# Macaron block in fp32 on one core: the low half of the gated product is subtracted on GpSimd instead of VectorE

## The chip, the cores and the metric

The kernel runs on one core of one Trainium2 chip. The metric is the device time of one execution in microseconds (us). Four engines work here: TensorE (PE) multiplies matrices, VectorE (DVE), ScalarE (ACT) and GpSimd (POOL) do the elementwise work, and SyncE (SP) issues the DMAs. Each runs its own instructions in order and waits on semaphores for the others.

## What is computed

Three sublayers over x of 4 batches by 512 tokens by 512 features, all in fp32:

```
x = x + 0.5 * ffn(layernorm(x))
x = x + scan_layer(layernorm(x))
x = x + 0.5 * ffn(layernorm(x))

ffn(x):         silu(x @ w_gate.T) * (x @ w_up.T) @ w_down.T            # hidden size 2048
scan_layer(x):  z = x @ W.T;  m_k[t] = lam_k * m_k[t-1] + z[t], k = 0..3
                h = z + sum_k eta_k * m_k;  gamma * layernorm(h) + beta
```

The product silu(gate) * up is called the gated product below; in the kernel it is the buffer `hid`.

## The kernel before

**Precision by two halves.** TensorE multiplies here in a rounded fp32 format. So each operand is split in a high half (the rounded copy, made on ScalarE) and a low half (the operand minus its high half, a subtraction), and each product is made of three matmuls: high by high, high by low, low by high. The helper `three` issues them (L718, L719, L720).

**Passes and steps.** A tile is one batch of 512 tokens. Each of the 4 tiles goes twice through the feed-forward network, which makes 8 passes, and a pass has 16 steps, one for each slice of 128 hidden units. In step g, with global number g, TensorE does in this order: the matmuls of gate(g) (12 of them), of up(g) (12), and then those of down(g-1) (12), that is, the down product of the slice before. Its PSUM banks `gate_ps` and `up_ps` are single. So up(g) waits until VectorE has read the bank of the step before (`hid_done`).

**The gated product.** After gate(g), ScalarE writes silu(gate) into `hid` (L409). After up(g), VectorE multiplies it by `up_ps` in place (L658, counts `hid_done`). ScalarE copies the result to the high half `hid_hi` (L426, counts `hid_hi_ready`), and VectorE subtracts to get the low half `hid_lo` (L667, counts `hid_lo_ready`). down(g) waits for `hid_lo_ready`. All three buffers have two slots.

**Work beside the steps.** `beside` tells what else a step carries:
- "ln" or "pre", 4 steps of a pass: VectorE takes the layer norm of 128 tokens each (statistics, then a reciprocal root by a one-column power on GpSimd, L448, then `norm`), turns them in blocks, and VectorE and ScalarE place the blocks in `row_t`. ScalarE then makes `xt_hi` (L391), VectorE `xt_lo` (L547), the operands of a later pass.
- "scan", 5 steps (s = 0 to 4), once for each tile: in steps s = 0 to 3, TensorE also makes one unit of z = x @ W.T, 12 matmuls into `aux_ps`, which come last in the step, after down(g-1). Their weights are split in the same step: ScalarE copies `w_scan_hi` (L418) right behind the silu, GpSimd subtracts `w_scan_lo` (L482). VectorE's part of unit s, the function `scan` (four recurrences L558, four accumulations L562, a transpose L590 and the placing), stands at the end of step s, and the gated product of step s+1 behind it.
- "post", 5 steps: the second half of the scan layer (norm, gamma, beta, residual) and the layer norm for the tile's second pass, with two one-column powers on GpSimd for each step (L454, L448).

In pass 0, ScalarE and GpSimd also split all the weights of the feed-forward network, a slice per step: GpSimd subtracts 128x1024 (`gu_lo`, L461) and 128x512 (`dn_lo`, L475). The halves are kept in HBM, and later passes fetch them.

**What sets the order.** All orders are written out by hand: the function `step(c)` of each engine is called by the same walk over all steps. SP issues the next weights of the FFN, and in scan steps also the next W (`load_w_scan`), which waits for `w_scan_lo_ready`.

Of the kernel before, what the change touches and what calls it, by code (L numbers as in the profile page):

```python
# [28 lines left out]
F32 = mybir.dt.float32  # L29
F32R = mybir.dt.float32r  # L30
ALU = mybir.AluOpType
# [16 lines left out]
def macaron_kernel(nc, x_in, w_ffn_in, w_scan_in, lam_logit_in, eta_in, gamma_in, beta_in, out):  # L48
# [18 lines left out]
    with ExitStack() as ctx:  # L67
        def sb(name, shape, dt=F32):
            return ctx.enter_context(nc.sbuf_tensor(name, shape, dt))

        def sem(name):
            return ctx.enter_context(nc.semaphore(name))
# [16 lines left out]
        hid = sb("hid", [P, 2, tokens])  # L89
        hid_hi = sb("hid_hi", [P, 2, tokens], F32R)  # L90
        hid_lo = sb("hid_lo", [P, 2, tokens], F32R)
# [43 lines left out]
        def parts(eng, c):  # L135


            split = P // 4 if c.beside == "post" and c.s < ST else P // 2
            return range(0, split, SQ) if eng is nc.vector else range(split, P, SQ)

        def place_rows(copy, parts):

            place_blocks(copy, parts, rows[:, 1, :], row_t, 0, blocks_placed)
# [40 lines left out]
        down_done = sem("down_done")  # L184
        silu_done = sem("silu_done")
        hid_done = sem("hid_done")
        hid_hi_ready = sem("hid_hi_ready")
        hid_lo_ready = sem("hid_lo_ready")
# [22 lines left out]
        def wait(eng, semaphore, n):  # L211

            if isinstance(n, int) and n <= 0:
                return
            eng.wait_ge(semaphore, n)

        def ln_count(f):

            return f - ST + 3
# [223 lines left out]
        @block.gpsimd  # L443
        def _(pool):
            def ln(f, u):

                pool.wait_ge(ln_ve_done, ln_count(f))
                pool.tensor_tensor(ln_rstd[:, u:u + 1], ln_ve[:, u:u + 1], minus_half[:, 0:1], ALU.pow  # L448
                                   ).then_inc(ln_rstd_done, 1)

            def post_norm(n):

                pool.wait_ge(post_ve_done, n + 1)
                pool.tensor_tensor(post_rstd[:, :], post_ve[:, :], minus_half[:, 0:1], ALU.pow  # L454
                                   ).then_inc(post_rstd_done, 1)

            def split_gu(t, slot, g):


                pool.wait_ge(gu_hi_ready, g + 1)  # L460
                pool.tensor_tensor(gu_lo[:, slot, :], w_ffn[:, t, 0:GU], gu_hi[:, slot, :].bitcast(F32),  # L461
                                   ALU.subtract).then_inc(gu_lo_ready, 1)

            def step(c):
                g = c.p * HT + c.t
                if c.beside in ("ln", "pre"):
                    ln(c.f, c.sp)
                if c.beside == "post" and c.s < ST:
                    post_norm(c.tile * ST + c.s)
                if isinstance(c.p, int) and c.p == 0:  # L470
                    if not (isinstance(c.t, int) and c.t == LAST):
                        split_gu(c.t + 1, (c.tp + 1) % 2, g + 1)

                    pool.wait_ge(dn_hi_ready, g + 1)
                    pool.tensor_tensor(dn_lo[:, c.tp, :], w_ffn[:, c.t, GU:GU + D],  # L475
                                       dn_hi[:, c.tp, :].bitcast(F32), ALU.subtract).then_inc(dn_lo_ready, 1)
                if c.beside == "post" and c.s < ST:
                    ln(c.f, c.sp)
                if c.beside == "scan" and c.s < DT:

                    pool.wait_ge(w_scan_hi_ready, c.tile * DT + c.s + 1)
                    pool.tensor_tensor(w_scan_lo[:, :], w_scan[:, :], w_scan_hi[:, :].bitcast(F32),  # L482
                                       ALU.subtract).then_inc(w_scan_lo_ready, 1)

            pool.memset(ident[:, :], 0.0).then_inc(ident_zero, 1)
            pool.memset(minus_half[:, :], -0.5).then_inc(ident_zero, 1)

            pool.wait_ge(ident_zero, 2)
            pool.affine_select(out=ident[:, :], in_=ident[:, :], compare_op=ALU.not_equal, fill=1.0, base=0,
                               pattern=[[-1, P]], channel_multiplier=1).then_inc(ident_ready, 1)  # L490
            for u in range(0, ST, 2):

                pool.wait_ge(ln_ve_done, u // 2 + 1)
                pool.tensor_tensor(ln_rstd[:, u:u + 2], ln_ve[:, u:u + 2], minus_half[:, u:u + 2], ALU.pow
                                   ).then_inc(ln_rstd_done, 1)
            pool.wait_ge(gate0_hi_ready, 1)
            pool.tensor_tensor(gu_lo[:, 0, 0:DT * P], w_ffn[:, 0, 0:DT * P], gu_hi[:, 0, 0:DT * P].bitcast(F32),
                               ALU.subtract).then_inc(gate0_lo_ready, 1)
            pool.wait_ge(gu_hi_ready, 1)
            pool.tensor_tensor(gu_lo[:, 0, DT * P:GU], w_ffn[:, 0, DT * P:GU],  # L500
                               gu_hi[:, 0, DT * P:GU].bitcast(F32), ALU.subtract).then_inc(gu_lo_ready, 1)
            walk(pool, step)

        @block.vector
        def _(dve):
            def stats(f, u, x):

                dve.bn_stats(ln_stats[:, u, :], x)

                dve.drain()  # L510
                dve.bn_aggr(ln_mv[:, u, :], ln_stats[:, u, :]).then_inc(ln_mv_done, 1)
                dve.wait_ge(ln_mv_done, f + 1)
                dve.tensor_scalar(ln_ve[:, u:u + 1], ln_mv[:, u, 1:2], EPS, None, ALU.add).then_inc(ln_ve_done, 1)

            def norm(f, u, x, row):


                dve.wait_ge(ln_rstd_done, ln_count(f))
                dve.tensor_scalar(row, x, ln_mv[:, u, 0:1], ln_rstd[:, u:u + 1], ALU.subtract,
                                  ALU.mult).then_inc(row_ready, 1)  # L520

            def turn_blocks(f):


                dve.wait_ge(row_ready, f + 1)

                dve.wait_ge(xt_hi_ready, f)
                dve.transpose(rows[:, 1, :], rows[:, 0, :]).then_inc(blocks_turned, 1)  # L528

                dve.drain()  # L530
# [97 lines left out]
            def add_y(p, b):  # L628


                dve.wait_ge(down_done, (p + 1) * HT)
                for q in range(ST):
                    x = x_tok[:, b * ST + q, :]
                    dve.scalar_tensor_tensor(x, down_ps[q][:, :], 0.5, x, ALU.mult, ALU.add).then_inc(y_added, 1)

            def step(c):
                g = c.p * HT + c.t
                if c.beside == "ln":

                    for b in (1,) if isinstance(c.p, int) and c.p == 0 else range(2, tiles):  # L640
                        dve.wait_ge(x_arrived[b], 16)
                if c.beside == "post":
                    post(c)
                if c.beside == "pre":

                    dve.drain()
                if c.beside in ("ln", "pre"):
                    x = x_tok[:, c.tile * ST + c.s, :]
                    stats(c.f, c.sp, x)
                    norm(c.f, c.sp, x, rows[:, 0, :])  # L650
                    turn_blocks(c.f)
                    place_rows(dve.tensor_copy, parts(nc.vector, c))
                if c.beside == "post" and c.s == ST:
                    split_xt(c, 1 - c.odd)

                dve.wait_ge(silu_done, g + 1)
                dve.wait_ge(up_done, g + 1)
                dve.tensor_tensor(hid[:, c.tp, :], hid[:, c.tp, :], up_ps[:, :], ALU.mult).then_inc(hid_done, 1)  # L658
                if c.beside == "post" and c.s < ST:

                    dve.drain()
                    stats(c.f, c.sp, x_tok[:, c.tile * ST + c.s, :])
                    split_xt(c, 1 - c.odd)

                dve.wait_ge(hid_hi_ready, g + 1)
                wait(dve, down_done, g - 1)
                dve.tensor_tensor(hid_lo[:, c.tp, :], hid[:, c.tp, :], hid_hi[:, c.tp, :].bitcast(F32),  # L667
                                  ALU.subtract).then_inc(hid_lo_ready, 1)
                if isinstance(c.t, int) and c.t == 0 and c.done is not None:
                    add_y(c.p - 1, c.done)  # L670
                if c.beside in ("ln", "pre"):
                    split_xt(c, 1 - c.odd)
                if c.beside == "scan" and c.s < DT:
                    scan(c)
# [180 lines left out]
```

## Time and profile before

| | |
|---|---|
| median of 3 runs | 1171.23 us (1169.49 to 1172.03) |
| the profiled execution | 1167.63 us, of which its span, first to last instruction, 1165.8 us |
| TensorE matmuls busy | 1121.0 us, 96% of the span |
| VectorE busy | 618.1 us, 53% |
| ScalarE busy | 372.5 us, 32% |
| GpSimd busy | 123.9 us, 11% |
| mean granted TensorE clock | 0.987 |

TensorE has work nearly always, so a change to another engine can win only what TensorE still waits for, and can lose wherever it makes TensorE wait anew.

### The profile page before, as it was taken

To read this page: it belongs to the slowest core of one execution; us is meant where nothing else is said; L and a number is where in the kernel's file an instruction comes from. 1 tells how busy PE (TensorE), PEld (TensorE's weight loads), DVE (VectorE), ACT (ScalarE), POOL (GpSimd) and SP (SyncE) were. 2 spreads that over 40 slices of the span, in tenths; PEclk is the share of its full clock that TensorE was granted. 3 is DMA by queue.
4 is the path that set the end of the run, shared out by engine and by line. 5 is a ranking of instruction groups with operands and counts; after the bars stand their busy time and mean duration, and the time that the engine had idled before them with its cause. 6 is when DMAs were issued, how large, how long until landed. Compare 5 with 4: busy or idle time off the path is not lost.

```text
span 1165.8 us, 14814 instructions
## 1 busy us (share of the span) xinstructions
PE 1121.0 (96%) x4860; PEld 914.1 (78%) x4860; DVE 618.1 (53%) x1244; ACT 372.5 (32%) x884; POOL 123.9 (11%) x118
## 2 busy tenths in 40 slices
PE   8998999989999999998999999999899998999998
PEld 7777888868877887886887888788688786887777
DVE  4842146788561115588946111559885588931112
ACT  4633324235251113332534111332362432521111
POOL 4434400101000000010100000001010010100000
PEclk9999999999999999998999999999899998999999
DMA  8889455444555546453544555553355452564544
GB/s 339 286 306 334 199 203 204 168 152 163 191 188 177 195 181 240 164 188 118 196 184 178 201 177 201 210 214 140 142 180 212 167 189 109 191 221 177 205 166 158
DMA packets 46564, 227.70 MB, mean 195 GB/s; under 512 B 5168, under 2 KB 5168, under 8 KB 30128
## 3 DMA queue, kind: packets, MB, share of 16 engines
q1 hardware_dynamic: 46368, 227.04, 53.1%
q8 instruction: 29, 0.48, 0.2%
q14 instruction: 23, 0.19, 0.0%
q10 hardware_dynamic: 144, 0.00, 0.0%
HBM read 197.66 MB, written 29.36 MB: 195 GB/s over the span
## 4 chain that ended last, share of the span: by engine, by line
PE 60%; DMA 15%; DVE 14%; issue 6%; POOL 2%; SPq 2%; ACT 1%; DVEq 0%; POOLq 0%; ACTq 0%
DMA gu<-gu_kept 13%; PE up_ps L718 7%; PE up_ps L719 7%; PE up_ps L720 7%; PE down_ps L718 7%; PE down_ps L720 7%; PE down_ps L719 6%; PE gate_ps L718 6%; PE gate_ps L719 6%; PE gate_ps L720 6%; DVE rows L558 5%; DVE scan_sum L562 4%; DVE scan_tok L132 2%; DMA gu_kept<-gu 2%; PE gate_ps L776 1%
## 5 line engine op out<-in xcount | busy, mean ns | idle before, releaser
L658 DVE TENSOR_TENSOR hid<-hid,up_ps 128x512 f32<-128x512 f32 x128 | 88.0, 687 | 380.2 <-PE up_ps L720 368.2
L718 PE MATMUL up_ps<-xt_hi,gu 128*128 128x512 f32 x512 | 204.4, 399 | 22.9 <-DVE hid L658 22.9
L718 PE MATMUL gate_ps<-xt_hi,gu 128*128 128x512 f32 x480 | 190.8, 397 | 13.2 <-DMA gu<-gu_kept 8.9
L719 PE MATMUL up_ps<-xt_lo,gu 128*128 128x512 f32 x512 | 203.1, 397 | 0.0
L720 PE MATMUL up_ps<-xt_hi,gu 128*128 128x512 f32 x512 | 202.9, 396 | 0.0
L409 ACT ACTIVATE hid<-gate_ps 128x512 f32<-128x512 f32 x128 | 76.7, 599 | 393.5 <-PE gate_ps L720 368.1
L718 PE MATMUL down_ps<-dn,hid_hi 128*128 128x512 f32 x512 | 199.8, 390 | 0.0
L719 PE MATMUL down_ps<-dn,hid_hi 128*128 128x512 f32 x512 | 199.4, 389 | 0.0
L720 PE MATMUL down_ps<-dn,hid_lo 128*128 128x512 f32 x512 | 199.2, 389 | 0.0
L719 PE MATMUL gate_ps<-xt_lo,gu 128*128 128x512 f32 x480 | 187.7, 391 | 0.0
L720 PE MATMUL gate_ps<-xt_hi,gu 128*128 128x512 f32 x480 | 187.6, 391 | 0.0
L426 ACT CAST hid_hi<-hid 128x512 fp32r<-128x512 f32 x128 | 79.5, 621 | 213.1 <-DVE hid L658 213.1
L667 DVE TENSOR_TENSOR hid_lo<-hid,hid_hi 128x512 fp32r<-128x512 f32 x128 | 92.2, 720 | 83.8 <-ACT hid_hi L426 83.8
L718 PEld LDWEIGHTS up_ps<-xt_hi,gu 128*128 128x128 f32 x512 | 98.2, 192 | 48.5 <-issue 28.4
L132 ACT COPY row_t<-rows 32x128 f32<-32x128 f32 x400 | 118.9, 297 | 28.0 <-DVE rows L528 22.4
L718 PEld LDWEIGHTS gate_ps<-xt_hi,gu 128*128 128x128 f32 x480 | 90.5, 189 | 43.3 <-DMA gu<-gu_kept 12.2
L720 PEld LDWEIGHTS up_ps<-xt_hi,gu 128*128 128x128 f32 x512 | 98.4, 192 | 21.0
L719 PEld LDWEIGHTS up_ps<-xt_lo,gu 128*128 128x128 f32 x512 | 98.4, 192 | 20.2
L718 PEld LDWEIGHTS down_ps<-dn,hid_hi 128*128 128x128 f32 x512 | 96.6, 189 | 20.2
L719 PEld LDWEIGHTS down_ps<-dn,hid_hi 128*128 128x128 f32 x512 | 96.5, 188 | 20.2
L720 PEld LDWEIGHTS down_ps<-dn,hid_lo 128*128 128x128 f32 x512 | 96.3, 188 | 20.1
L720 PEld LDWEIGHTS gate_ps<-xt_hi,gu 128*128 128x128 f32 x480 | 90.5, 189 | 19.2
(68 smaller groups left out, 946.1 us busy)
## 6 DMA issues: line engine op xcount, KB each, us to landing
gu<-gu_kept SPq DMA_DIRECT2D x112, 1024.0 KB, 5.9
dn<-dn_kept SPq DMA_DIRECT2D x112, 512.0 KB, 3.5
gu_kept<-gu SPq DMA_DIRECT2D x16, 1024.0 KB, 8.3
w_ffn<-w_ffn_in SPq DMA_DIRECT2D x15, 768.0 KB, 6.4
dn_kept<-dn SPq DMA_DIRECT2D x16, 512.0 KB, 3.0
w_scan<-w_scan_in SPq DMA_DIRECT2D x16, 256.0 KB, 3.9
x_tok<-x_in SPq DMA_DIRECT2D x3, 1024.0 KB, 10.3
out<-x_tok SPq DMA_DIRECT2D x3, 1024.0 KB, 6.3
```

The source lines that it names most:

```text
L132: last = copy(dst[b:b + SQ, :, at + a:at + a + SQ], blocks[a:a + SQ, :, b:b + SQ])
L409: act.activation(hid[:, c.tp, :], gate_ps[:, :], ACT.Silu).then_inc(silu_done, 1)
L426: act.copy(hid_hi[:, c.tp, :], hid[:, c.tp, :]).then_inc(hid_hi_ready, 1)
L558: return dve.tensor_tensor_scan(rows[:, k % 2, :], lam[:, k:k + 1].to_broadcast([P, tokens]), z, 0.0, ALU.mult, ALU.add)
L562: return dve.scalar_tensor_tensor(total, rows[:, k % 2, :], eta[:, k:k + 1], to, ALU.mult, ALU.add)
L658: dve.tensor_tensor(hid[:, c.tp, :], hid[:, c.tp, :], up_ps[:, :], ALU.mult).then_inc(hid_done, 1)
L667: dve.tensor_tensor(hid_lo[:, c.tp, :], hid[:, c.tp, :], hid_hi[:, c.tp, :].bitcast(F32), ALU.subtract).then_inc(hid_lo_ready, 1)
L718: pe.matmul(dst, a_hi, b_hi, start=start, stop=False)
L719: pe.matmul(dst, a_hi, b_lo, start=False, stop=False)
L720: return pe.matmul(dst, a_lo, b_hi, start=False, stop=stop)
L776: pe.matmul(dst[:, cols], gu[:, c.tp, w[k]], xt_hi[:, c.odd, k, cols], start=k == 0 and gu is gu_hi, stop=False)
```

## The change

The subtraction that gives `hid_lo` is taken out of VectorE's step and put in GpSimd's step with the same two waits: behind the weight splits of pass 0, ahead of the second layer-norm power of a "post" step, and ahead of the subtraction for `w_scan_lo` of a "scan" step. Nothing else differs. There are 128 such subtractions.

```
--- before.py
+++ after.py
@@ -474,6 +474,11 @@
                     pool.wait_ge(dn_hi_ready, g + 1)
                     pool.tensor_tensor(dn_lo[:, c.tp, :], w_ffn[:, c.t, GU:GU + D],
                                        dn_hi[:, c.tp, :].bitcast(F32), ALU.subtract).then_inc(dn_lo_ready, 1)
+
+                pool.wait_ge(hid_hi_ready, g + 1)
+                wait(pool, down_done, g - 1)
+                pool.tensor_tensor(hid_lo[:, c.tp, :], hid[:, c.tp, :], hid_hi[:, c.tp, :].bitcast(F32),
+                                   ALU.subtract).then_inc(hid_lo_ready, 1)
                 if c.beside == "post" and c.s < ST:
                     ln(c.f, c.sp)
                 if c.beside == "scan" and c.s < DT:
@@ -661,11 +666,6 @@
                     dve.drain()
                     stats(c.f, c.sp, x_tok[:, c.tile * ST + c.s, :])
                     split_xt(c, 1 - c.odd)
-
-                dve.wait_ge(hid_hi_ready, g + 1)
-                wait(dve, down_done, g - 1)
-                dve.tensor_tensor(hid_lo[:, c.tp, :], hid[:, c.tp, :], hid_hi[:, c.tp, :].bitcast(F32),
-                                  ALU.subtract).then_inc(hid_lo_ready, 1)
                 if isinstance(c.t, int) and c.t == 0 and c.done is not None:
                     add_y(c.p - 1, c.done)
                 if c.beside in ("ln", "pre"):
```

GpSimd's program in the five scan steps of the first tile and the start of the post steps, before the change (x4 is four in a row; each row ends with the semaphores that it waits for):

```order
L482 TENSOR_TENSOR w_scan_lo<-w_scan,w_scan_hi 128x512 [waits w_scan_hi_ready] x4
L454 TENSOR_TENSOR ln_rstd<-ln_ve,minus_half 128x1 [waits post_ve_done]
L448 TENSOR_TENSOR ln_rstd<-ln_ve,minus_half 128x1 [waits ln_ve_done]
L454 TENSOR_TENSOR ln_rstd<-ln_ve,minus_half 128x1 [waits post_ve_done]
L448 TENSOR_TENSOR ln_rstd<-ln_ve,minus_half 128x1 [waits ln_ve_done]
```

The same place with the change:

```order
L480 TENSOR_TENSOR hid_lo<-hid,hid_hi 128x512 [waits down_done,hid_hi_ready]
L487 TENSOR_TENSOR w_scan_lo<-w_scan,w_scan_hi 128x512 [waits w_scan_hi_ready]
...
L480 TENSOR_TENSOR hid_lo<-hid,hid_hi 128x512 [waits down_done,hid_hi_ready]
L487 TENSOR_TENSOR w_scan_lo<-w_scan,w_scan_hi 128x512 [waits w_scan_hi_ready]
L480 TENSOR_TENSOR hid_lo<-hid,hid_hi 128x512 [waits down_done,hid_hi_ready]
L454 TENSOR_TENSOR ln_rstd<-ln_ve,minus_half 128x1 [waits post_ve_done]
L480 TENSOR_TENSOR hid_lo<-hid,hid_hi 128x512 [waits down_done,hid_hi_ready]
L448 TENSOR_TENSOR ln_rstd<-ln_ve,minus_half 128x1 [waits ln_ve_done]
```

Each subtraction for `w_scan_lo` now stands behind the `hid_lo` of its own step, and so does each layer-norm power of the post steps (L448).

VectorE's program from the gated product of a scan step to that of the next (the recurrences of L558 are listed as SCALAR_TENSOR_TENSOR here), before:

```order
L658 TENSOR_TENSOR hid<-hid,up_ps 128x512 [waits up_done,silu_done]
L667 TENSOR_TENSOR hid_lo<-hid,hid_hi 128x512 [waits down_done,hid_hi_ready]
L558 SCALAR_TENSOR_TENSOR rows<-lam,aux_ps 128x512 [waits z_done,rows_arrived]
...
L590 STREAM_TRANSPOSE row_t<-scan_sum 128x512
L132 COPY scan_tok<-row_t 32x4x32 x8
L658 TENSOR_TENSOR hid<-hid,up_ps 128x512 [waits up_done,silu_done]
```

and with the change:

```order
L663 TENSOR_TENSOR hid<-hid,up_ps 128x512 [waits up_done,silu_done]
L563 SCALAR_TENSOR_TENSOR rows<-lam,aux_ps 128x512 [waits z_done,rows_arrived]
...
L595 STREAM_TRANSPOSE row_t<-scan_sum 128x512
L132 COPY scan_tok<-row_t 32x4x32 x8
L663 TENSOR_TENSOR hid<-hid,up_ps 128x512 [waits up_done,silu_done]
```

The recurrence follows the gated product directly; its own wait, for TensorE's z, is the same.

## Rows read from the trace of the kernel before

**Rows 1.** The page: busy us of each engine, its share of the span, instructions.

```profile
PE 1121.0 (96%) x4860; PEld 914.1 (78%) x4860; DVE 618.1 (53%) x1244; ACT 372.5 (32%) x884; POOL 123.9 (11%) x118
```

**Rows 2.** Who waited for whom: us in total, times, longest us.

```profile
PE up_ps L718 <- DVE hid L658: 22.9, 13, 3.9
```

**Rows 3.** DVE timeline, first scan stage: start us, us, line, operation, idle before.

```profile
205.27 0.69 DVE L658 TENSOR_TENSOR hid<-hid,up_ps 128x512 f32<-128x512 f32 x1 [5.40 <-PE up_ps L720]
...
210.71 2.33 DVE L558 TENSOR_TENSOR_SCAN rows<-lam,aux_ps 128x512 f32<-128x512 f32 x2 [3.37 <-PE aux_ps L720]
...
222.08 0.69 DVE L658 TENSOR_TENSOR hid<-hid,up_ps 128x512 f32<-128x512 f32 x1
...
224.07 2.32 DVE L558 TENSOR_TENSOR_SCAN rows<-lam,aux_ps 128x512 f32<-128x512 f32 x2
...
234.42 0.69 DVE L658 TENSOR_TENSOR hid<-hid,up_ps 128x512 f32<-128x512 f32 x1
...
259.10 0.69 DVE L658 TENSOR_TENSOR hid<-hid,up_ps 128x512 f32<-128x512 f32 x1
```

**Rows 4.** PE timeline, same stage: first matmul of some products.

```profile
207.72 0.39 PE L718 MATMUL aux_ps<-xt_hi,w_scan_hi 128*128 128x512 f32 x1
210.44 0.39 PE L718 MATMUL gate_ps<-xt_hi,gu 128*128 128x512 f32 x1
247.59 0.47 PE L718 MATMUL up_ps<-xt_hi,gu 128*128 128x512 f32 x1 [1.18 <-DVE hid L658]
250.43 0.39 PE L718 MATMUL down_ps<-dn,hid_hi 128*128 128x512 f32 x1
259.94 0.77 PE L718 MATMUL up_ps<-xt_hi,gu 128*128 128x512 f32 x1 [3.90 <-DVE hid L658]
265.19 0.47 PE L718 MATMUL down_ps<-dn,hid_hi 128*128 128x512 f32 x1
```

**Rows 5.** ACT and POOL timelines, same stage.

```profile
222.80 0.62 ACT L426 CAST hid_hi<-hid 128x512 fp32r<-128x512 f32 x1 [0.39 <-DVE hid L658]
...
203.67 1.29 POOL L482 TENSOR_TENSOR w_scan_lo<-w_scan,w_scan_hi 128x512 fp32r<-128x512 f32 x1 [10.18 <-ACT w_scan_hi L418]
```

**Rows 6.** PE by stretches: busy (matmuls), granted clock, DMA share, GB/s.

```profile
91.00:95.40 4.40, 4.40 (x12) 0.61 0.68 199
...
259.90:265.20 5.30, 5.26 (x13) 0.50 0.04 19
```

**Rows 7.** PE timeline in pass 0.

```profile
90.98 0.57 PE L718 MATMUL gate_ps<-xt_hi,gu 128*128 128x512 f32 x1 [2.98 <-POOL gu L461]
95.43 0.40 PE L718 MATMUL up_ps<-xt_hi,gu 128*128 128x512 f32 x1
```

**Rows 8.** DVE, ACT and POOL timelines in pass 0.

```profile
26.17 1.66 DVE L667 TENSOR_TENSOR hid_lo<-hid,hid_hi 128x512 fp32r<-128x512 f32 x1 [0.69 <-ACT hid_hi L426]
...
35.26 0.69 DVE L658 TENSOR_TENSOR hid<-hid,up_ps 128x512 f32<-128x512 f32 x1
...
37.33 0.69 DVE L547 TENSOR_TENSOR xt_lo<-row_t,xt_hi 128x512 f32 x1
...
45.23 0.69 DVE L658 TENSOR_TENSOR hid<-hid,up_ps 128x512 f32<-128x512 f32 x1
...
35.98 0.62 ACT L426 CAST hid_hi<-hid 128x512 fp32r<-128x512 f32 x1 [2.55 <-DVE hid L658]
...
26.00 1.29 POOL L475 TENSOR_TENSOR dn<-w_ffn,dn 128x512 fp32r<-128x512 f32 x1
```

**Rows 9.** ACT, POOL, DVE and PE timelines, last post steps of the first tile.

```profile
292.26 0.62 ACT L426 CAST hid_hi<-hid 128x512 fp32r<-128x512 f32 x1
...
297.89 0.62 ACT L391 CAST xt_hi<-row_t 128x512 fp32r<-128x512 f32 x1
...
293.05 0.93 POOL L448 TENSOR_TENSOR ln_rstd<-ln_ve,minus_half 128x1 f32<-128x1 f32 x1 [5.43 <-DVE ln_ve L513]
...
300.71 1.98 PE L776 MATMUL gate_ps<-xt_hi,gu 128*128 128x512 f32 x8
```

More of the change, by code:

```diff
@@ L476, in step @@
                                        dn_hi[:, c.tp, :].bitcast(F32), ALU.subtract).then_inc(dn_lo_ready, 1)
+                pool.wait_ge(hid_hi_ready, g + 1)
+                wait(pool, down_done, g - 1)
+                pool.tensor_tensor(hid_lo[:, c.tp, :], hid[:, c.tp, :], hid_hi[:, c.tp, :].bitcast(F32),
+                                   ALU.subtract).then_inc(hid_lo_ready, 1)
                 if c.beside == "post" and c.s < ST:
@@ L663, in step @@
                     split_xt(c, 1 - c.odd)
[L665 to L668, printed above, removed]
                 if isinstance(c.t, int) and c.t == 0 and c.done is not None:
```

## The prediction

> **What bounds the kernel now.** I read the page first: TensorE is busy for 96% of the span, GpSimd for 11% [rows 1]. So outside its few waits the kernel is TensorE's own time. The view of waits comes next. The one wait that VectorE causes is that of up for the gated product, 22.9 us in 13 places, the longest 3.9 us [rows 2]. The timelines say where: nearly all of it lies in the four scan stages, one for each tile. There VectorE needs 222.08 to 234.42, 12.34 us, from one gated product to the next [rows 3], while TensorE has 48 matmuls. Twelve matmuls take 2.72 us (207.72 to 210.44 [rows 4]), so 48 take 10.88. TensorE runs ahead, and at the end of the stage it waits 1.18 and then 3.90 us [rows 4]. Everywhere else a step is 36 matmuls, 8.16 us, and VectorE is done in time.
>
> A second thing hangs on that last wait. The up that follows it takes 259.94 to 265.19, 5.25 us in place of 2.72 [rows 4], since the granted clock is 0.50 of full there, the 1.2 GHz level [rows 6]. So idling for 3.90 us cost 2.53 us more. After 2.98 us of idling in pass 0 the next twelve took 90.98 to 95.43, 4.45 us, or 1.73 more [rows 7], at a mean granted clock of 0.61 [rows 6]. After 1.18 us they took 247.59 to 250.43, only 0.12 more [rows 4].
>
> **The change, part by part.**
>
> *The subtraction itself.* On VectorE it takes 0.69 us. For GpSimd the nearest row is the same shape and operation, w_scan_lo: 1.29 us [rows 5]. In a plain step that changes nothing: hid_lo(g) is ready some 3.0 us after up(g) (0.27 + 0.72 + 0.62 + 0.08 + 1.29, from the steps below), and down(g) starts only after down(g-1), gate(g+1) and up(g+1), 8.16 us. If that cover were gone, 0.6 us per step would be lost, 77 us in 128 steps. The only step without cover is the last of all, where just down(126), 2.72 us, lies between: I add 0.4 us (bounds 0 and 0.6).
>
> *The scan stages: a new loop of waits.* This is the term that decides. On GpSimd, w_scan_lo(n) now stands behind hid_lo(n), which waits for hid_hi(n), which waits for the gated product hid(n). Before, it started right behind the silu, before up was done. TensorE needs it for z(n), VectorE needs z(n) for its recurrences, and these stand ahead of hid(n+1). So the loop hid(n), hid_hi, hid_lo, w_scan_lo, z(n), scan(n), hid(n+1) is closed, and nothing in it overlaps:
> - hid(n) to the start of hid_hi 0.72, hid_hi 0.62 [rows 3, 5]; about 0.08 for a semaphore, hid_lo 1.29, w_scan_lo 1.29 [rows 5], 0.05 to TensorE: 4.05 us
> - z(n) to the first recurrence: 207.72 to 210.71, 2.99 us [rows 3, 4]
> - the recurrences and their tail to the next gated product: 224.07 to 234.42, 10.35 us [rows 3]
>
> The sum is 17.39 in place of 12.34: 5.05 more. TensorE, which waits for w_scan_lo with z(n), has behind it only gate and up of the next step and down of this one. They take only 8.16 of the 14.67 us (0.27 + 10.35 + 4.05) between one z and the next, so TensorE idles some 6.5 us ahead of each z. By the rows above a wait of 2.98 us cost 1.73 and one of 3.90 cost 2.53. The bounds are thus 0 and 2.72 (all twelve at half clock), and I take 2.3, between the two measured. The Trainium skill (TensorE: Matmul & The Clock Gate, What's actually happening) says that "the default state is throttled, and activity releases the throttle". By that rule each of these z pays, with it the sum has the 2.3 and without it the 2.3 is missing; the trace agrees in two places of the two with a wait that long.
>
> For a tile, against hid(S4), the last product of the stage:
> - first unit: hid(S0) at 205.27, so z can start at 209.32, not 207.72: +1.6 [rows 3, 4]
> - the first run of recurrences takes 210.71 to 222.08, 11.37, where the second takes 10.35 [rows 3]. The next w_scan_lo runs beside the first one on GpSimd, and does so no more: about -0.95
> - units 1 to 3: 3 x (5.05 + 2.3) = +22.05
>
> That is +22.7. Then something comes back. The up behind hid(S4) found TensorE idle for 3.90 us before; now gate, up, down and gate (10.88) fill the time behind z(3) but for some 0.5 us. So it runs at full clock: -2.4.
>
> SP's load of the next W waits for w_scan_lo too, and the fetch of gu stands behind it. Both are later by the same shift, but ScalarE wants the new W only after the next gate, 2.72 us after the end of z, and I cost them at 0. If the load took longer than z and that gate together, the rest would be added to each unit; nothing in the rows speaks for it.
>
> *Post stage.* The layer-norm power now waits for hid_lo. In the last post step hid_hi ends at 292.88; hid_lo would end at 294.25 and the power, 0.93, at 295.2, where it ended at 293.98: 1.2 later. The two steps before I estimate at 0.5 each and the first at 0.15, between 0 and that 1.2. VectorE begins post work 1.25 sooner, being rid of one subtraction and the wait ahead of it (222.08 to 224.07 less 0.69 and 0.05 [rows 3]), and has 0.3 of waiting to give. xt_hi was done at 298.51, 2.2 us ahead of the next pass's gate at 300.71 [rows 9]; but TensorE is now 2.4 ahead. -2.2 + 2.4 + 2.3 - 1.25 - 0.3 gives a new wait of 0.9 us (bounds 0 and 2.0).
>
> *Pass 0.* When GpSimd's dn_lo had started (26.00 to 27.29), VectorE's hid_lo took 1.66 and ended 0.54 after it [rows 8]. So a VectorE operation with two inputs in SBUF is held until GpSimd's is done. With the change, GpSimd subtracts from about 36.7 to 38.0, just when VectorE wants xt_lo (37.33) [rows 8]: it ends at 38.5, 0.5 late, although hid_lo is gone. Steps here take 35.26 to 45.23, 9.97 us, so VectorE is the bound for three of them: +1.5 us (bounds 0 and 5).
>
> Sum: 4 x (22.7 - 2.4 + 0.9) + 1.5 + 0.4 = 86.7 us. The profiled execution took 1167.63, so it would be 1254.3. It is 3.6 below the median of the runs; the same sum on 1171.23 gives **1258**.
>
> **The rivals.**
> - *The same loop at full clock.* If the granted clock held through 6.5 us of idling, 12 x 2.3 = 27.6 would go: 1230. Two long waits speak against it. Chance 0.08.
> - *VectorE's relief wins (the other side).* Its step in the scan stage is 12.34 us, 1.99 of it from hid to the recurrences [rows 3]. Without hid_lo and its wait it would be 11.1, nearly TensorE's 10.88, and the waits of 4.1 us and the clock loss of 2.4 would go in each tile: 26 us less, 1145. The point that decides is whether w_scan_lo(n) is ready when down(n-1) ends: in the first unit 2.45 us after hid(n) starts (205.27 to 207.72 [rows 3, 4]), while it comes 4.05 after at best, and in the later ones TensorE is ahead of VectorE altogether. Chance 0.04.
> - *Nothing measurable.* That needs z(n) to lie off VectorE's path, yet the recurrences start 0.27 after it [rows 3, 4]. Chance 0.02.
> - *Blocking everywhere.* There are 48 steps with layer-norm or post work. A blocked operation was prolonged by about 1 us (1.66 for 0.69). TensorE bears about 4.6 us of lateness at the product (5.44 less 0.69, less latency); five steps at 1.2 to 2 use up 6 to 10. With 11 such runs of steps 1.4 to 5 us each come on top: 1273 to 1313. The Trainium skill (SBUF — State Buffer, Who interferes with whom) has the rule: whichever of the two engines starts first keeps the shared port for its whole instruction. That gives this rival its mechanism; row 26.17 agrees. Against it: most steps have only xt_lo at that moment. Chance 0.08.
>
> **How the numbers follow.** The main case has 0.78. Its own range comes from its bounds: the clock 1.73 to 2.72 for each z (-7, +5), low clock at the first z (+7), the post wait (-4, +4), pass 0 (-2, +3). For 8 in 10 I take 1240 to 1273, which leaves out the full clock, the faster case and most of the last rival. 0.2% is about what a measurement can tell from no change. Slower by over that: 0.78 + 0.08 + 0.08 = 0.94; within it 0.02; faster 0.04.
>
> **What would show it.** In the changed profile: w_scan_lo on GpSimd right behind hid_lo, starting about 2.7 us after the product's start, not behind the silu; VectorE waiting for aux_ps in all 16 units, some 6.4 us in the first of a tile and 8.6 in the other three; gated products 19 to 20 us apart in the scan stages; a granted clock near 0.5 in z; TensorE's matmuls of up no longer waiting 3.9 us for hid; its idle ahead of aux_ps some 84 us in total; everything outside the scan stages within 2 us per pass. I am wrong if the products are 17.4 apart (clock), if GpSimd's hid_lo is far from 1.29 us, or if up waits for hid in the ln, pre and post steps.

## The result, and the profile after

The changed kernel takes 1256.59 us (median of 4 runs, 1253.54 to 1258.54), the kernel before 1171.53 (4 runs). The ratio is 1.0727, with a 95% interval of 1.0701 to 1.0753: 7.3% slower, 85.1 us. The forecast was 1258, within 1240 to 1273. The profiled execution took 1258.54 us with a span of 1256.7, against 1167.63 and 1165.8 before.

The page of the changed kernel, span and busy time:

```profile
span 1256.7 us, 14896 instructions
PE 1144.6 (91%) x4860; PEld 928.2 (74%) x4860; DVE 548.7 (44%) x1116; ACT 371.8 (30%) x884; POOL 284.1 (23%) x246
```

TensorE issues the same 4860 matmuls, yet is busy 23.6 us longer [rows 1]: part of them ran slower. The rest of the 90.9 us that the span grew, 67.3, is idle time. TensorE's waits (us in total, times, longest) say before what:

```profile
PE aux_ps L718 <- POOL w_scan_lo L487: 67.3, 13, 6.4
PE aux_ps L718 <- issue: 14.4, 3, 6.7
PE gate_ps L718 <- DMA gu<-gu_kept: 13.2, 18, 1.9
PE gate_ps L718 <- POOL gu L461: 5.3, 3, 3.5
PE up_ps L718 <- DVE hid L663: 3.4, 6, 0.9
...
PE down_ps L718 <- POOL hid_lo L480: 0.2, 1, 0.2
```

The first two rows are one thing: TensorE ahead of z, 16 times, 81.7 us together. Where the trace did not find the releaser it wrote "issue", with waits of the same lengths (one of 1.4 and two of 6.3 and 6.7 us). The wait for hid, 22.9 us before [rows 2], is down to 3.4. The subtraction that was moved delays TensorE directly in one place of 128, by 0.2 us; its cost is in what stands behind it.

GpSimd's timeline in the first scan stage (start us, us, line, operation, idle before):

```profile
210.92 1.28 POOL L480 TENSOR_TENSOR hid_lo<-hid,hid_hi 128x512 fp32r<-128x512 f32 x1 [6.36 <-ACT hid_hi L426]
212.16 1.26 POOL L487 TENSOR_TENSOR w_scan_lo<-w_scan,w_scan_hi 128x512 fp32r<-128x512 f32 x1
228.43 1.26 POOL L480 TENSOR_TENSOR hid_lo<-hid,hid_hi 128x512 fp32r<-128x512 f32 x1 [15.01 <-ACT hid_hi L426]
229.65 1.26 POOL L487 TENSOR_TENSOR w_scan_lo<-w_scan,w_scan_hi 128x512 fp32r<-128x512 f32 x1
```

w_scan_lo stands right behind hid_lo each time. It was not its own input that held it: before, it started at 203.67, even ahead of the step's product at 205.27 [rows 3, 5]. VectorE's timeline, gated products and recurrences:

```profile
209.50 0.69 DVE L663 TENSOR_TENSOR hid<-hid,up_ps 128x512 f32<-128x512 f32 x1 [4.40 <-PE up_ps L720]
216.64 2.33 DVE L563 TENSOR_TENSOR_SCAN rows<-lam,aux_ps 128x512 f32<-128x512 f32 x2 [6.46 <-PE aux_ps L720]
...
227.01 0.69 DVE L663 TENSOR_TENSOR hid<-hid,up_ps 128x512 f32<-128x512 f32 x1
236.37 2.33 DVE L563 TENSOR_TENSOR_SCAN rows<-lam,aux_ps 128x512 f32<-128x512 f32 x2 [8.67 <-PE aux_ps L720]
...
246.75 0.69 DVE L663 TENSOR_TENSOR hid<-hid,up_ps 128x512 f32<-128x512 f32 x1
...
266.67 0.69 DVE L663 TENSOR_TENSOR hid<-hid,up_ps 128x512 f32<-128x512 f32 x1
...
285.44 0.69 DVE L663 TENSOR_TENSOR hid<-hid,up_ps 128x512 f32<-128x512 f32 x1
```

The first two products are 17.51 us apart, where it was 16.81; the next are 19.74, 19.92 and 18.77 apart, where they were 12.34 [rows 3]. VectorE, the bound of this stage before, now waits for z in each unit: some 6.5 us in the first of a tile and 7.7 to 8.9 in the other three. TensorE by stretches (busy, granted clock, DMA share, GB/s), the idle time ahead of a z, that z, and what follows it:

```profile
224.60:230.90 6.30, 0.10 (x1) 0.86 0.26 83
230.90:236.10 5.20, 5.14 (x12) 0.52 0.65 255
236.10:238.90 2.80, 2.80 (x14) 1.00 0.00 0
...
270.60:274.80 4.20, 4.17 (x13) 0.66 0.00 0
286.20:289.10 2.90, 2.83 (x12) 1.00 1.00 402
```

After 6.26 us of idling z runs at a granted clock of 0.52 and takes 5.14 us instead of 2.72; the last z of this tile had a mean clock of 0.66 and took 4.2. The up at 286.2, the first of the post steps, is at full clock now, where it was at 0.50 [rows 6].

### The profile page after: what moved, and what is told of

Its sections match the earlier page's. It is cut to its first block, busy times and chain, and to the rows that moved or that the text cites. A ratio compares the mean times of both kernels' runs of the same rounds, so it can differ in the third digit from the quotient of the medians.

```text
span 1256.7 us, 14896 instructions
## 1 busy us (share of the span) xinstructions
PE 1144.6 (91%) x4860; PEld 928.2 (74%) x4860; DVE 548.7 (44%) x1116; ACT 371.8 (30%) x884; POOL 284.1 (23%) x246
## 4 chain that ended last, share of the span: by engine, by line
PE 55%; issue 18%; DMA 15%; DVE 6%; POOL 4%; SPq 1%; ACT 1%; POOLq 0%; DVEq 0%; ACTq 0%
DMA gu<-gu_kept 13%; PE up_ps L718 6%; PE up_ps L720 6%; PE up_ps L719 6%; PE gate_ps L718 6%; PE down_ps L720 6%; PE down_ps L718 6%; PE down_ps L719 6%; PE gate_ps L719 5%; PE gate_ps L720 5%; DMA gu_kept<-gu 2%; POOL w_scan_lo L487 2%; POOL hid_lo L480 1%; DVE rows L563 1%; DVE scan_sum L567 1%
## 5 line engine op out<-in xcount | busy, mean ns | idle before, releaser
L480 POOL TENSOR_TENSOR hid_lo<-hid,hid_hi 128x512 fp32r<-128x512 f32 x128 | 169.3, 1323 | 901.1 <-ACT hid_hi L426 901.1
L718 PE MATMUL gate_ps<-xt_hi,gu 128*128 128x512 f32 x480 | 192.7, 401 | 18.9 <-DMA gu<-gu_kept 13.2
L718 PE MATMUL up_ps<-xt_hi,gu 128*128 128x512 f32 x512 | 200.0, 391 | 3.5 <-DVE hid L663 3.4
L720 PE MATMUL up_ps<-xt_hi,gu 128*128 128x512 f32 x512 | 199.2, 389 | 0.0
L719 PE MATMUL up_ps<-xt_lo,gu 128*128 128x512 f32 x512 | 199.2, 389 | 0.0
L563 DVE TENSOR_TENSOR_SCAN rows<-lam,aux_ps 128x512 f32<-128x512 f32 x64 | 76.4, 1214 | 130.3 <-PE aux_ps L720 129.2
L718 PEld LDWEIGHTS gate_ps<-xt_hi,gu 128*128 128x128 f32 x480 | 92.0, 192 | 49.3 <-DMA gu<-gu_kept 14.5
L718 PEld LDWEIGHTS up_ps<-xt_hi,gu 128*128 128x128 f32 x512 | 96.2, 188 | 25.9 <-issue 6.2
L718 PE MATMUL aux_ps<-xt_hi,w_scan_hi 128*128 128x512 f32 x64 | 37.8, 591 | 81.7 <-POOL w_scan_lo L487 67.3
L718 PEld LDWEIGHTS down_ps<-dn,hid_hi 128*128 128x128 f32 x512 | 96.1, 188 | 20.5 <-POOL hid_lo L480 0.6
L720 PEld LDWEIGHTS up_ps<-xt_hi,gu 128*128 128x128 f32 x512 | 96.1, 188 | 20.1
L719 PEld LDWEIGHTS up_ps<-xt_lo,gu 128*128 128x128 f32 x512 | 96.3, 188 | 19.8
```

Of the source, the lines that this page charges most:

```text
L480: pool.tensor_tensor(hid_lo[:, c.tp, :], hid[:, c.tp, :], hid_hi[:, c.tp, :].bitcast(F32), ALU.subtract).then_inc(hid_lo_ready, 1)
L563: return dve.tensor_tensor_scan(rows[:, k % 2, :], lam[:, k:k + 1].to_broadcast([P, tokens]), z, 0.0, ALU.mult, ALU.add)
L718: pe.matmul(dst, a_hi, b_hi, start=start, stop=False)
L719: pe.matmul(dst, a_hi, b_lo, start=False, stop=False)
L720: return pe.matmul(dst, a_lo, b_hi, start=False, stop=stop)
```

## The experiments

Seven kernels, in two series, each timed beside the kernel before on the same chip (there 1168.8 us in both series). The ratio is what to compare, as the chips differ by 0.2%.

**1. The order on GpSimd alone.** The changed kernel with w_scan_lo subtracted first:

```
+                if c.beside == "scan" and c.s < DT:
+                    pool.wait_ge(w_scan_hi_ready, c.tile * DT + c.s + 1)
+                    pool.tensor_tensor(w_scan_lo[:, :], ...).then_inc(w_scan_lo_ready, 1)
                 pool.wait_ge(hid_hi_ready, g + 1)
                 wait(pool, down_done, g - 1)
                 pool.tensor_tensor(hid_lo[:, c.tp, :], ...).then_inc(hid_lo_ready, 1)
                 if c.beside == "post" and c.s < ST:
                     ln(c.f, c.sp)
-                if c.beside == "scan" and c.s < DT:
-                    ...
```

> The changed kernel, but in scan steps GpSimd subtracts w_scan_lo ahead of hid_lo. If the loss comes from w_scan_lo queued behind hid_lo (my theory), the loop opens: z is ready early again, the step of VectorE in a scan stage falls to about 11.1 us, the wait of 3.9 us and the clock loss of 2.5 us behind it go, and the time is that of the kernel before, 1171.5, less 4 x 6.5 = 26, plus the 3.7 us that pass 0 lost and up to 4 us of waits for gu: 1147 to 1155. If the loss is that of the slower engine, or of the shared port blocking VectorE in all the steps, the place of w_scan_lo changes little: above 1230.

Measured: 1146.11 us (6 runs), ratio 0.9805 (0.9780 to 0.9831). The expectation of 1147 to 1155 was worked from 1171.5 us; the ratio times that is 1148.7. So all 128 subtractions are on the slower engine, and the kernel is 2% faster than before and, by the two ratios, 8.6% faster than the changed one. The whole loss, and more, was the order of two instructions. TensorE's wait for hid, 22.9 us before [rows 2], is 9.4 here. VectorE's timeline in its scan stage:

```profile
223.80 0.69 DVE L663 TENSOR_TENSOR hid<-hid,up_ps 128x512 f32<-128x512 f32 x1
224.41 2.32 DVE L563 TENSOR_TENSOR_SCAN rows<-lam,aux_ps 128x512 f32<-128x512 f32 x2
...
234.78 0.69 DVE L663 TENSOR_TENSOR hid<-hid,up_ps 128x512 f32<-128x512 f32 x1
...
245.75 0.69 DVE L663 TENSOR_TENSOR hid<-hid,up_ps 128x512 f32<-128x512 f32 x1
...
256.71 0.69 DVE L663 TENSOR_TENSOR hid<-hid,up_ps 128x512 f32<-128x512 f32 x1
```

The recurrences follow the product at once, and products are 10.97 us apart: near the 10.88 of TensorE's 48 matmuls.

**2 and 3. One part of the steps at a time.** Both split the steps between the two engines; a wait for the subtraction of the step before keeps their count in order. In the second, the condition is the opposite.

```
+                if not (c.beside == "scan"):                  # on pool
+                    wait(pool, hid_lo_ready, g)
                     pool.wait_ge(hid_hi_ready, g + 1)
                     ...
+                if c.beside == "scan":                        # on dve
+                    wait(dve, hid_lo_ready, g)
+                    dve.wait_ge(hid_hi_ready, g + 1)
+                    ...
```

> hid_lo stays on VectorE in the five scan steps of each tile and goes to GpSimd in all the others, 108 of 128. Theory: nearly all of the loss lies in the scan stages, so the time is 1171.5 plus 3.7 (pass 0) plus 0 to 4: 1173 to 1180. Rival (blocking everywhere): the 108 moved subtractions carry the loss, above 1200.

> The complement: hid_lo goes to GpSimd only in the five scan steps of each tile, ahead of w_scan_lo as in the change. Theory: 1171.5 + 4 x 20.7 = 1254, range 1248 to 1258, with gated products 19.7 us apart. Rival (blocking everywhere): below 1200.

Measured: with the 108 steps outside the scan stages moved, 1173.05 us (12 runs), ratio 1.0035 (1.0012 to 1.0059), some 4 us slower. With only the 20 scan steps moved, 1254.13 us (4 runs), ratio 1.0718 (1.0683 to 1.0753), the loss of the whole change. The two parts add up to it within their intervals, and the rival of blocking everywhere falls.

**4. The clock by itself.** The changed kernel, with useless matmuls in TensorE's idle time:

```
+                    wait(pe, z_bank_free, unit - 1)
+                    if c.s > 0:
+                        for r in range(22):
+                            pe.matmul(aux_ps[c.sp][:, :], xt_hi[:, 1 - c.odd, r % DT, 0:P],
+                                      xt_hi[:, 1 - c.odd, r % DT, :], start=True, stop=True)
                     pe.wait_ge(w_scan_lo_ready, unit + 1)
-                    wait(pe, z_bank_free, unit - 1)
```

> The changed kernel, with 22 more matmuls of no use (they write the bank that z then overwrites) ahead of each z of units 1 to 3, in the time in which TensorE idles there (6.3 us; they take 5.0 at full clock). Theory: the 2.3 us per unit beyond the queueing is TensorE's clock, which falls while it idles; kept busy, it stays at full clock, z takes 2.7 in place of 5.1 us, products are 17.4 us apart, and the time is 1256.6 - 12 x 2.3 = 1229 (1226 to 1234). Rival: the z is slow for another reason, or the filler only shifts the wait: 1256 or more.

Measured: 1227.39 us (4 runs), ratio 1.0507 (1.0470 to 1.0543). 264 matmuls more, and 29 us faster by the medians (26 by the ratios, which allow for the chip). VectorE's products are 17.54 and 17.51 us apart, as in a loop at full clock (mean of the 12 steps 17.57):

```profile
225.27 0.69 DVE L663 TENSOR_TENSOR hid<-hid,up_ps 128x512 f32<-128x512 f32 x1
232.42 2.33 DVE L563 TENSOR_TENSOR_SCAN rows<-lam,aux_ps 128x512 f32<-128x512 f32 x2 [6.46 <-PE aux_ps L720]
...
242.81 0.69 DVE L663 TENSOR_TENSOR hid<-hid,up_ps 128x512 f32<-128x512 f32 x1
...
260.32 0.69 DVE L663 TENSOR_TENSOR hid<-hid,up_ps 128x512 f32<-128x512 f32 x1
```

and TensorE's stretch with its z is at full clock, where it was at 0.52:

```profile
229.70:232.40 2.70, 2.70 (x14) 1.00 0.84 261
```

**5. Pass 0 left alone.** As the first experiment, with hid_lo of pass 0 on VectorE (the split of experiments 2 and 3, on the condition that p is 0).

> As e1_wscan_first (w_scan_lo ahead of hid_lo), but in pass 0 hid_lo is subtracted on VectorE as before. Theory: pass 0 loses 3.7 us to the move, so this saves that: 1142 to 1144 against 1146.1 of e1_wscan_first. Rival: the later start of pass 0 is given back elsewhere, and it is 1146 again.

Measured: 1146.85 us (5 runs), ratio 0.9819 (0.9792 to 0.9846). A miss: no faster than the first experiment. In the profiles pass 0 was indeed shorter (its last product at 146.76 us in place of 149.65), but at the end of the first tile's post steps the two were level (the next pass's first product at 301.72 and 301.74). The traces of the two show where most of the 2.9 us went. TensorE waited twice for gu, 0.62 us in all, where it did not in the first experiment. And in the second scan unit VectorE was 0.5 us longer, since one accumulation was held beside w_scan_lo:

```profile
226.65 1.24 DVE L569 SCALAR_TENSOR_TENSOR scan_sum<-rows,eta,scan_sum 128x512 f32<-128x512 f32 x1
...
226.06 1.29 POOL L481 TENSOR_TENSOR w_scan_lo<-w_scan,w_scan_hi 128x512 fp32r<-128x512 f32 x1 [1.38 <-ACT w_scan_hi L418]
```

In the first experiment the same accumulation takes 0.72. So the up behind the stage waited 1.98 us instead of 1.50, and its twelve matmuls took 4.11 us instead of 2.80. Whether that is so in every execution is not shown: one profile of each was taken, and the whole difference is within what the measurement tells apart.

**6. One more subtraction in the loop.**

```
                     pool.wait_ge(w_scan_hi_ready, c.tile * DT + c.s + 1)
+                    pool.tensor_tensor(w_scan_lo[:, :], ..., ALU.subtract).then_inc(once_done, 1)
+                    pool.wait_ge(once_done, c.tile * DT + c.s + 1)
                     pool.tensor_tensor(w_scan_lo[:, :], ..., ALU.subtract).then_inc(w_scan_lo_ready, 1)
```

> The changed kernel, with the subtraction for w_scan_lo done twice in each of the 16 scan units (the same result written again, and only the second announced). Theory: it lies in the closed loop, so all of its 1.26 us is paid, with about 0.05 for the wait between the two: 16 x 1.3 = 21 more, 1277 (1274 to 1281). Rival: the loop has slack on GpSimd's side, and less than 10 us are added.

Measured: 1276.26 us (4 runs), ratio 1.0919 (1.0888 to 1.0951). Against the changed kernel's 1.0727 that is 0.0192 of 1168.8, 22 us, for 16 subtractions of 1.26 and a wait of about 0.08 each (21.4). That the sum fits so well is in part luck. TensorE's wait ahead of z did grow by the whole of it: from 1.48 to 2.83 us (means) in the first unit of a tile, from 6.31 to 7.68 in the other three. But the matmuls behind the waits changed too. The z of the first and of the second unit of the first tile (busy, granted clock, DMA share, GB/s):

```profile
214.50:218.90 4.40, 4.40 (x13) 0.61 0.83 292
234.80:239.60 4.80, 4.80 (x13) 0.57 0.73 277
```

The first z of a tile, which had taken 2.8 us, now took 4.2 to 4.4 in three of the four tiles (and 2.85 in one, after a wait of the same length): +4.5 us in sum. The twelve later ones took 4.6 in the mean, where they had taken 5.0: -5.4. The two nearly cancel, and the products of the later units are 20.6 us apart, 0.9 more and not 1.3.

**7. Only the scan stages moved, in the good order.** As the first experiment, with GpSimd subtracting hid_lo in scan steps only.

> hid_lo goes to GpSimd only in the five scan steps of each tile, behind w_scan_lo; everywhere else it stays on VectorE. Theory: the gain of e1_wscan_first comes from the scan stages alone, so this has all of the gain and none of what pass 0 loses: 1140 to 1145. Rival: part of the gain comes from VectorE's relief in the post and pre steps, and this is slower than e1_wscan_first, 1148 or more.

Measured: 1145.12 us (5 runs), ratio 0.9792 (0.9769 to 0.9815). That is at the upper end of the expected range and 3 us below the rival's. It and the first experiment are the best versions, and they can't be told apart. So the gain lies in the scan stages; moving the other 108 neither adds to it nor, measurably, takes from it.

## Why the prediction was right, by its steps

**The loop.** Forecast: 4.05 us from a product to z, 2.99 to the recurrences, 10.35 to the next product. Measured in the first unit: 209.50 to 216.64, 7.14 us for the first two, and 10.37 for the third. With the clock the forecast was 19.7 us per step; the mean of all 12 steps is 19.72. Experiment 4 splits it: 17.6 for the queueing, which had been put at 17.39, and the rest for the clock. Experiment 1 shows that opening the loop takes all of it away, experiment 6 that TensorE waits for the whole of an addition to it.

**The clock.** 2.3 us per z was taken between two rows of before. Forecast in sum 27.6 us, measured by taking it away 26 to 29. In the trace of the changed kernel the twelve z took 60.4 us, which is 27.8 more than at full clock. The forecast counted two long waits in the trace of before, but there were five: the last up of the other three tiles waited 3.9 us as well, and all five cost 1.7 to 2.5 us. So there was more support than it claimed. The size is a mean, though, and does not follow from the length of the wait: after waits of 6.1 to 6.7 us a z lost 1.5 to 2.6 us, and after the 7.6 to 8.0 us of experiment 6 it lost 1.6 to 2.2. That 2.3, read off waits of 2.98 and 3.90 us, held for waits of 6.3 is in part luck.

**What comes back.** Two sentences of the forecast were about gains inside the loss: no w_scan_lo beside the first recurrences (10.37 where it was 11.37), and no slow up behind the stage. The up at 286.27 waited 0.42 us and ran at full clock (2.83 us), as forecast.

**The post stage was wrong.** Forecast: a new wait of 0.9 us per tile at the next pass's gate. There was none. In the first tile xt_hi ends at 324.00 and the gate starts at 324.67: a slack of 0.7 in place of the 2.2 before. The direction (slack shrinks) was right. Three of the terms were right too: against hid(S4), the last product of the scan stage, TensorE's gate came 2.4 us sooner (forecast 2.4), the first product of the post stage 1.24 sooner (forecast 1.25), and from the last step's product to the start of xt_hi it took 8.00 us, where it was 6.83, so 1.2 later (forecast 1.2). The step at fault is the estimate for the three steps before the last. It was 0.15, 0.5 and 0.5 us more, less 0.3 of waiting; they took 7.63, 8.58 and 8.57 us, where they had taken 8.25, 8.85 and 8.46, so 0.8 less in sum. Why is open. VectorE's lighter load in these steps does not explain it by itself: in experiment 2, where hid_lo is moved in the post steps and not in the scan steps, the three take 25.6 to 26.1 us in the four tiles, and before they took 25.5 to 25.8. In experiment 3, where it is the other way round, they take 24.8 to 25.3, and with the whole change 24.8 to 25.0.

**Pass 0 was too small.** Forecast +1.5 us (within its bounds of 0 and 5); the last product of pass 0 came 3.7 later (151.12 for 147.39). The mechanism was the forecast one, xt_lo held until GpSimd's subtraction is done, but it took more in each step, and something followed from it:

```profile
37.59 1.32 DVE L552 TENSOR_TENSOR xt_lo<-row_t,xt_hi 128x512 f32 x1 [1.35 <-ACT xt_hi L391]
...
37.06 1.30 POOL L480 TENSOR_TENSOR hid_lo<-hid,hid_hi 128x512 fp32r<-128x512 f32 x1 [3.00 <-ACT hid_hi L426]
```

GpSimd started at 37.06, 0.16 after hid_hi's end, not 0.1, and xt_lo, which takes 0.69 in [rows 8], lasted 1.32. Three steps took 10.80, 10.44 and 10.52 us where they took 9.97: 1.9 us. That term was nearly right; what the forecast had left out came behind it. Then TensorE's later wait for gu grew from 2.98 [rows 7] to 3.53 us, and the twelve matmuls behind it took 5.29 instead of 4.45, at a mean granted clock of 0.50 instead of 0.61 [rows 6].

**The end.** Forecast 0.4 us, measured a wait of 0.15: the bounds held it.

**Blocking everywhere.** The rival's mechanism is real and its price nearly nothing. In the groups by line of the changed kernel, all 28 xt_lo of the ln and pre steps were held:

```profile
L552 DVE TENSOR_TENSOR xt_lo<-row_t,xt_hi 128x512 f32 x28 | 36.4, 1301 | 37.6 <-ACT xt_hi L391 37.6
L552 DVE TENSOR_TENSOR xt_lo<-row_t,xt_hi 128x512 fp32r<-128x512 f32 x16 | 11.0, 684 | 4.9 <-ACT xt_hi L391 4.9
```

1.30 us in place of 0.69, 0.6 longer in each. The rival had put it at about 1 us. Outside pass 0 that stays inside the 4.6 us that TensorE bears, as experiment 2 shows: 4 us more for 108 moved steps, about as much as pass 0 alone had lost.

**The sum.** From the first product of a scan stage to that of the next pass, the shift grew by 19.8, 21.6, 20.6 and 20.8 us in the four tiles (24.01 - 4.23 in the first), 82.8 together; 84.8 was forecast. Of the 90.9 us of span the other 8 are pass 0 (3.7) and longer waits for gu (13.2 us, 8.9 before). These varied between 9.7 and 13.0 us over the profiles of the other kernels too, and why was not tried. In the forecast that part was 1.9, some 6 too little, and the post wait of 3.6 that did not come made up for more than half of that. So the main term was right by its mechanism and its size, while the closeness of the total (85.1 us by the medians and 90.9 in the profile, 86.7 forecast) is in part luck.

**Slips of the working.** Up's wait for hid is not the only one that VectorE causes: TensorE also waited 3.7 us in 3 places, at the start of the kernel, for `scan_tok`. And the faster rival takes 4.1 us of waits per tile without saying from what, where the rows have 1.18 + 3.90. Neither enters the sum.

## What to carry to other kernels

Before moving an instruction to an idle engine, look at what stands behind it in that engine's order and whether that work was ready earlier: an engine with 11% load turned into the longest wait of the kernel because one instruction that waits late was put ahead of one that is needed early. Moving the same work behind the early one gave a gain of 2%, although the engine takes nearly twice as long for it. Where a new wait of TensorE is longer than those that the trace shows as harmless, add the matmuls that run slow behind it; here that was a third of the loss. Treat its size as a range: in these traces twelve matmuls lost 1.7 us behind a wait of 1.91 us and 0.1 behind one of 2.87.

## What was not expected of the hardware

264 matmuls without any use made a kernel 26 to 29 us faster, by keeping the granted clock at 1.00 instead of 0.52 in the matmuls that count. When VectorE and GpSimd each subtract two operands from SBUF, the one that starts first keeps its time and the other pays. In the 28 ln and pre steps GpSimd started first: its hid_lo took 1.3 us, and VectorE's xt_lo went from 0.69 to 1.30. In 11 of the 16 post steps with an xt_lo, VectorE started first, by 0.04 to 0.26 us: its xt_lo kept 0.68 us, and GpSimd's hid_lo took 1.57 to 1.78 instead of the 1.26 to 1.30 of the other 117. One such pair:

```profile
308.63 0.68 DVE L552 TENSOR_TENSOR xt_lo<-row_t,xt_hi 128x512 fp32r<-128x512 f32 x1
...
308.69 1.77 POOL L480 TENSOR_TENSOR hid_lo<-hid,hid_hi 128x512 fp32r<-128x512 f32 x1 [5.69 <-ACT hid_hi L426]
```
